# Two largest-value reductions over pairs of tiles, each written as one MAX8 per tile

## The reference

```python
def _top_p_attention(X, W1, W2, W3):
    q = X @ W1.T @ W2.T
    k = X @ W3.T
    probs = softmax(q @ k.T, axis=-1)
    idx = argsort(-probs); sp = take_along_axis(probs, idx); cs = cumsum(sp)
    keep_sorted = cs - sp < 0.9
    ...
    A = probs * mask
    return A / maximum(A.sum(-1), 1e-12)
R = S + eye(N); R = R / R.sum(-1)
for n in range(2):
    A = _top_p_attention(Xa, W1, W2, W3)
    Xf = R @ Xf
    Xa = A @ Xa
    Z = Z + Xf @ U1[n].T + Xa @ U2[n].T
h = layernorm(x + Z) * ln_g + ln_b
out = layernorm(x + h)
```

## Time and profile before

| | us |
|---|---|
| runs of the kernel before, median of 3 | 1433.92 |
| lowest and highest of them | 1429.52, 1434.26 |
| the profiled execution, its own time | 1431.37 |
| its span, first to last instruction | 1429.3 |
| VectorE busy in it | 1281.5 (90%) |
| TensorE busy | 1228.1 (86%) |
| ScalarE busy | 930.7 (65%) |
| GpSimd busy | 340.5 (24%) |

### The profile page before, as it was taken

How to read it: one execution, slowest core, us unless ns; L and a number is a source line. 1 busy time by engine, 2 the same in 40 slices (tenths; PEclk the granted TensorE clock), 3 DMA queues, 4 the chain that set the end, 5 groups by cost and what they waited for, 6 DMA issues and landing times.

```text
span 1429.3 us, 29789 instructions
## 1 busy us (share of the span) xinstructions
PE 1228.1 (86%) x9162; PEld 1036.5 (73%) x9162; DVE 1281.5 (90%) x7010; ACT 930.7 (65%) x2026; POOL 340.5 (24%) x584
## 2 busy tenths in 40 slices
PE   7999999999997979897989796919895885929896
PEld 3677777777785968887888786818784775828796
DVE  5998989998976888899989989999998999999995
ACT  5888887788757565756575555636764746646764
POOL 0112322232201331312141220202332222212242
PEclk9999999999998989998999898969998897969998
DMA  5000000000021541412132132211312041211421
GB/s 205 2 1 2 2 2 2 2 2 2 2 97 49 193 145 38 156 49 97 55 139 96 50 103 91 97 48 49 145 50 96 2 145 49 94 52 50 145 49 49
DMA packets 16599, 96.49 MB, mean 68 GB/s; under 512 B 1251, under 2 KB 8930, under 8 KB 9730
## 3 DMA queue, kind: packets, MB, share of 16 engines
q1 hardware_dynamic: 16384, 94.14, 18.7%
HBM read 92.43 MB, written 1.70 MB: 66 GB/s over the span
## 4 chain that ended last, share of the span: by engine, by line
PE 44%; DVE 37%; ACT 11%; issue 5%; POOL 1%; DVEq 1%; DMA 0%; SPq 0%; ACTq 0%; POOLq 0%
PE bank L623 24%; DVE cand L841 13%; PE bank L602 11%; DVE junkC L898 8%; PE bank L554 5%; ACT E L696 4%; DVE E L1241 2%; ACT blkT L721 2%; ACT cand L691 2%; DVE sub L1064 2%; DVE E L1261 1%; PE bank L638 1%; DVE junkS L898 1%; DVE slots L963 1%; ACT S L696 1%
## 5 line engine op out<-in xcount | busy, mean ns | idle before, releaser
L721 ACT ACTIVATE blkT<-bank 128x512 f32<-128x512 f32 (+1 forms) x728 | 406.4, 565 | 284.7 <-PE bank L602 280.7
L841 DVE MAX8 cand<-E 128x8 f32<-128x32 f32 (+1 forms) x2992 | 404.2, 192 | 41.8 <-ACT E L674 26.4
L623 PEld LDWEIGHTS bank<-X,blkT 128*128 128x128 f32 x2704 | 329.1, 191 | 104.1 <-ACT blkT L721 71.8
L623 PE MATMUL bank<-X,blkT 128*128 128x129 f32 (+1 forms) x2704 | 375.9, 281 | 10.3 <-ACT blkT L721 9.1
L602 PE MATMUL bank<-ident,S 128*128 128x128 f32 x1560 | 242.0, 275 | 17.4 <-POOL S L451 15.6
L602 PE MATMUL bank<-ident,E 128*128 128x128 f32 x1144 | 183.0, 285 | 81.0 <-DVE E L1261 81.0
L898 DVE SCALAR_TENSOR_TENSOR junkC<-cand,st 128x128 f32<-128x128 f32 (+2 forms) x390 | 236.0, 613 | 2.0
L623 PE MATMUL bank<-YF,blkT 128*128 128x128 f32 x1352 | 192.7, 287 | 36.1 <-ACT blkT L721 36.1
L623 PEld LDWEIGHTS bank<-YF,blkT 128*128 128x128 f32 x1352 | 171.6, 199 | 68.7 <-ACT blkT L721 57.6
L554 PE MATMUL bank<-kT,Q 64*128 64x512 f32 (+1 forms) x728 | 197.0, 613 | 8.7 <-ACT E L674 8.4
L602 PEld LDWEIGHTS bank<-ident,E 128*128 128x128 f32 x1144 | 143.7, 148 | 83.3 <-DVE E L1261 82.1
(11 more groups left out here) (226 smaller groups left out, 1336.6 us busy)
## 6 DMA issues: line engine op xcount, KB each, us to landing
S<-in_adj_dram SPq DMA_DIRECT2D x50, 1663.5 KB, 6.8
S<-in_adj_dram SPq DMA_DIRECT2D x2, 1455.6 KB, 8.5
X<-in_x_dram SPq DMA_DIRECT2D x6, 256.0 KB, 5.4
out_dram<-H SPq DMA_DIRECT2D x1, 1408.0 KB
S<-in_adj_dram SPq DMA_DIRECT2D x2, 194.9 KB, 9.7
u_in<-in_L_gnn_U_dram SPq DMA_DIRECT2D x4, 64.0 KB, 9.6
out_dram<-H SPq DMA_DIRECT2D x1, 128.0 KB
w_in<-in_L_gnn_W_dram SPq DMA_DIRECT2D x2, 32.0 KB, 2.1
```

What stands on the lines that cost most here:

```text
L623: m = pe.matmul(bank[int(u.acc)][:, 0:width], blkT[:, slot, b * P:(b + 1) * P], rhs[:, j, 0:width], start=(j == 0), stop=(j == NT - 1))
L721: act.activation(blkT[:, slot, 0:w], BLK[early][slot][:, 0:w], ACT.Copy).then_inc(blk_done, 1)
L841: v.max(cand[:, par, xx, 8 * r:8 * r + 8], E[where_e[self.s, self.p]][:, xx, r * w:min((r + 1) * w, N)]).then_inc(s_max, 1)
```

## The change

Each of the two TENSOR_REDUCE operations over a pair becomes two MAX8 operations, one for each of its tiles, which write the eight largest values of the same strided view to a new small buffer (`best`, `lowest`); the first of the eight is what the reduction gave. `negm` is then made from `best[:, :, 0]` in place of from itself, with a wait for both MAX8; what read `FLOOR` now reads `lowest[:, :, 0]`, directly at the comparison in step 0 and at the joining in step 1. The wait after line 957 is for the second MAX8. The views that are read are the same ones: 2 x 16 values in step 0, 2 x 104 in step 1, each 32 bytes from the next. The reduction at line 969, over `slots`, stays.

```diff
@@ close()
                     dve.wait_ge(s_max, self.total)
                     top = cand[:, par, :, 0:NC[self.s]].rearrange("p x (n k) -> p x n k", k=8)[:, :, :, 0]
-                    v.tensor_reduce(negm[:, par, :], top, AX.X, ALU.max).then_inc(s_max, 1)
-                    dve.wait_ge(s_max, self.total + 1)
-                    v.tensor_scalar(negm[:, par, :], negm[:, par, :], -1.0, None, ALU.mult).then_inc(max_ready, 1)
+                    for xx in range(2):
+                        v.max(best[:, xx, :], top[:, xx, :]).then_inc(s_max, 1)
+                    dve.wait_ge(s_max, self.total + 2)
+                    v.tensor_scalar(negm[:, par, :], best[:, :, 0], -1.0, None, ALU.mult).then_inc(max_ready, 1)
@@ search()
                 runs = cand[:, par, :, 0:n].rearrange("p x (n k) -> p x n k", k=8)
-                link(v.tensor_reduce(two(FLOOR), runs[:, :, :, 7], AX.X, ALU.max))
+
+                for xx in range(2):
+                    ins = v.max(lowest[:, xx, :], runs[:, xx, :, 7])
+                    if xx:
+                        link(ins)
+                    else:
+                        link.post(ins)
...
-                    link.post(v.tensor_tensor(two(FLOOR), two(FLOOR), two(FLOOR2), ALU.max))
+                    link.post(v.tensor_tensor(two(FLOOR), lowest[:, :, 0], two(FLOOR2), ALU.max))
...
-                link.post(v.tensor_tensor(two(PICK), two(TSTAR), two(FLOOR), ALU.is_le))
+                link.post(v.tensor_tensor(two(PICK), two(TSTAR), two(FLOOR) if F else lowest[:, :, 0], ALU.is_le))
```

More of the change, by code:

```diff
@@ L283, in gnn_top_p_kernel @@
         st = sb("st", [P, 64])
+        best = sb("best", [P, 2, 8])
+        lowest = sb("lowest", [P, 2, 8])
         mv = sb("mv", [P, NT])
```

## The result

| | before | after |
|---|---|---|
| median of 22 runs each, us | 1431.29 | 1435.29 |
| lowest and highest, us | 1427.67, 1435.04 | 1432.68, 1440.91 |
| ratio, 95% interval | | 1.0027 [1.0017, 1.0037] |
| the profiled execution, us | 1431.37 | 1433.35 |
| its span, us | 1429.3 | 1431.4 |

The change makes the kernel slower by 0.27%, 3.9 us with an interval of 2.4 to 5.3. That is within the bound of 0.5%, the forecast's case, at more than twice the forecast's size of 1.7 us. The forecast's time of 1434.3 lies closer to 1435.29 than its step does to the measured one: it stood on a zero of 1432.65, and the 22 runs put the kernel before at 1431.29. That two errors of opposite sign met there is luck.

What follows compares the result with a forecast made beforehand. It took a three-engine ring (VectorE, ScalarE, TensorE) with little slack to bound step 0, VectorE step 1 from 1045 us. +1.2 (step 0) and +0.5 (step 1) gave +1.7 us on 1432.65: 1434.3 us, range 1429.0 to 1440.0.

Steps and rivals of the forecast that it cites:

- the bound: Whole kernel: a difference of 0.5%, 7.2 us, counts as no change; chance of staying within it 0.84.
- a zero of 1432.65: Starting time for the forecast: the middle between the profiled execution's 1431.37 us and the three runs' median of 1433.92.
- a ring without slack: Step 0's chain through VectorE, ScalarE and TensorE, none with much slack: 20 places at +0.06 us, +1.2 us.
- the upper end: Stepped reads cost MAX8 what they cost the reduction: 0.090 us for 16 values, 0.254 for 104; chance 0.53.
- The rival with the contiguous price: MAX8 doesn't pay for the step: 0.076 us for 16 values, 0.169 for 104; sum -0.4 us, chance 0.27.
- Nine places in step 1: Replaced operations on step 1's path: 0.45 us becomes 0.51, +0.06 each, +0.5 us in all.
- the 23 beside the path: Replaced operations off the chain, 6 in step 0 and 17 in step 1, costed at nothing.
- the covers' end: Upper sum if the cover over the 23 operations beside the path were gone: +3.1 us.
- Late code: VectorE's branches in step 1: 65 more instructions redraw the waits for code; slower case +10.9 us, chance 0.11.
- the main cases: Stepped price (0.53) and contiguous price (0.27), both nearly always within 0.5%, even with 3 us either way for code positions.
- eight places from 820 us on: Step 1 waits behind branches, 5.35 us above the branches' own price; the change makes them a new draw.
- none over 0.9: Step 0's waits behind branches, called even: 6.9 us in eight places, each at most 0.9; argued against late code.

Runs made afterwards that it cites:

- measured by itself: Kernel before, with three unread MAX8 and three reductions at its end for each size (16 to 104 values) and step (1 to 8): 1475.74 us.
- the one with step 0 alone: The change in step 0 only, step 1 keeping its two reductions, against the kernel before: 1433.61 us, ratio 1.0013.
- the one with the code put back: Changed kernel with 62 instructions left out of arms that never run, against the kernel before: 1434.57 us, ratio 1.0022.
- The added MAX8: Changed kernel plus unread MAX8 at each place, six in step 0 or four in step 1: 1450.74 and 1447.34 us, ratios 1.0133 and 1.0107 against before.
- three places of the code: Changed kernel as is, 62 never-run instructions fewer, 64 more: 1435.29, 1434.57, 1437.55 us; kernel before as is, 62 more, 64 more: 1431.29, 1433.54, 1428.57 us.

## Why the prediction was right, and where it wasn't

The outcome is the forecast's: no change within the bound, and a loss, not a gain. Its mechanism, a second instruction at the full stepped price on a ring without slack, is what the profiles show, for 2.1 to 2.5 of the 3.9 us.

*The price of a stepped MAX8.* Taken at the upper end, 0.254 and 0.090 us; measured by itself 0.245 and 0.087, and in place 0.62 us to `negm`, as forecast. The rival with the contiguous price has fallen.

*Step 0 on the ring.* Forecast +0.12 us a pair, measured +0.13, in the changed kernel, in the one with step 0 alone and in the one with the code put back. This was the choice that mattered, to believe the chain against TensorE's 28.54 busy us of 28.91.

*Nine places in step 1, and the 23 beside the path at nothing.* This term was somewhat too small. The added MAX8 show step 0's places at full price, 26 x 0.065 = 1.7 us at most (the pairs' distances show 1.3), and step 1's at about half: 26 x 0.06 / 2 = +0.8 us in place of +0.5, an estimate. The sum becomes +2.1 to +2.5 us. I had given the covers' end as +3.1.

*The zero.* 1432.65 was 1.4 us too high, which hid most of the shortfall of 2.2 us in the time itself. The median of three runs, 1433.92, was 2.6 above that of 22.

*Late code.* I called it a draw, gave it 3 us either way inside the main cases, and counted eight places from 820 us on. It moves the time (-3.0 us by 64 instructions that never run), and the waits whose change shows in the pairs behind them are among those from 820 us on. Leaving out the place near 492 us, where the chain runs over TensorE, holds up as well: its wait shrank from 6.3 to 1.7 us in the changed kernel, and pair 15 gained nothing on pair 13. Wrong was "none over 0.9" for step 0, where the trace has a wait by issue of 1.1 us, at 57 us (line 1261). The clock was in no rival, though it is lower in part of step 1 already.

*What stays open.* Measured are +3.9 us, 2.4 to 5.3; the instructions explain 2.1 to 2.5. The rest may be the code's place, the clock, or both: with the change in three places of the code the kernel is +3.9, +3.2 and +6.0 us, without it 0, +1.6 and -3.0. The means of three differ by 4.8 us, with a spread within each three of some 2 us. All three with the change came out slower than all three without it, though the intervals of +3.2 and +1.6 overlap; whether the change's own price is 2 or 4 us I can't say. Which branch meets which wait I couldn't tell from where the instructions stand. The Trainium skill's account (Runtime: NRT & Kernel Launch, Instruction fetch mechanics) is a fetch when a taken branch's target isn't in the current window. Waits that move when only unexecuted instructions are added agree with it, and no run here shows the fetch itself.

## What to carry to other kernels

Before replacing an operation, ask what it reads: two instructions over the same scattered view pay the same read and one more fixed price, while laying the data so that the reads are neighbours made VectorE's reductions and ScalarE's exponentials faster at once, and that kernel was 0.25% faster here. An engine that is busy for 99% of a period need not be its bound; follow the chain through one period, and test it by adding a few unread instructions. In a program with branches, a difference of 0.2% can be where the code lies: move it with instructions that never run before explaining it. And before reading a shift between two profiles as an instruction's price, lay their granted clocks side by side: a low stretch of 3 us went with later pairs 1.7 us behind.

## What the runs showed that I had not expected

64 instructions in an arm that never runs made a kernel of 1431 us faster by 3.0 us, and the changed one, if anything, slower. MAX8 and a reduction to one value cost the same within 2 ns at every size from 16 to 104 values but for the first of a series, whose next start comes some 19 ns later for MAX8 and 8 ns sooner for the reduction. ScalarE was slower over two values of every eight than over neighbours by (668 - 456) / 208 = 1.0 ns a value, and VectorE over five of eight by nothing. Two executions of one kernel differed by 3 us at one point of step 1, where one had the lower clock and the other not.
